# Class order of the pixels: from the ScalarE operands of a two-layer convolution kernel to its PSUM writes

## The chip, the cores and the metric

The kernel runs on one core of one Trainium2 chip. TensorE multiplies and writes PSUM, VectorE and ScalarE do elementwise work, GpSimd (POOL) and the SyncE queue (SP) move data. The metric is the device time of one execution in microseconds (us); lower is better.

## The reference

The input `x` is 16 images of 512 channels of 64 by 64 pixels, float32. Two layers follow each other, each `x = x + layer(groupnorm(x))`.

```python
# layer 0, on g = groupnorm(x)
corrs = [jnp.sum(g * shifted(g, di, dj), axis=1) for di in range(5) for dj in range(5)]
gs = jnp.stack(corrs, axis=1)                       # 25 products of a pixel with its 5x5 neighbours
gs = gs / jnp.sqrt(jnp.sum(gs * gs, axis=1, keepdims=True) + 1e-6)
feat = jnp.concatenate([g, gs], axis=1)             # 512 + 25 channels
x = x + relu(jnp.einsum('bchw,oc->bohw', feat, W) + bias)
# layer 1: each channel plane is max-pooled with one of the windows 1, 3, ... 13 that a small
# network on the plane means selects, two neighbouring windows are mixed, and x is added
```

## The kernel before

**Tiling.** An image lies in SBUF as 4 channel tiles (`CT`) of 128 partitions by 4096 pixels. Layer 0 goes through it in 8 chunks (`CH`) of 8 rows, 512 pixels each. Layer 1 starts when all images are through (about 2630 us) and is not touched by the change.

**One chunk of layer 0.** ScalarE normalises the chunk twice for each channel tile (`normalise`, L506 into the float32 `g32`, L508 into the float16 `gh`), and VectorE makes the low part `gl` = `g32` - `gh` (`low_parts`, L713). TensorE multiplies in three float16 products (high by high, high by low, low by high):

- `gram` (L1056): for each pair of image rows, 128 pixels as the weights and 256 pixels (4 rows) as the moving operand, 12 products that accumulate in a PSUM bank. Four such blocks belong to a chunk. VectorE masks the result to the band of neighbours (`mask`, L726, L731, L732) into `bq`.
- `turn_blocks` (L1114): transposes of four masked blocks, which ScalarE copies out (`after`, L528).
- `picks` (L1101): 48 small products that collect the 25 correlations from `bq`. `norm` (L1123) sums their squares, ScalarE takes the root (L537), VectorE divides (`descriptor`, L745, L749), POOL splits in high and low, and SP regroups the result with small DMAs into `tpair`.
- `conv` (L1079 to L1081): 48 products of 512 columns, 12 for each of the four output tiles. `tail` (L1134): 8 products of 256 columns that add the 25 descriptor channels of the chunk before to the same PSUM banks.
- ScalarE adds the bias and clips (`conv_out`, L520), VectorE adds the result to `x` and takes its statistics (`residual`, L738, L740).

**Order of the pixels.** A pair of rows has 128 pixels. In natural order their index is `(r, j, k)`: row, eight groups, pixel in the group. In class order it is `(k, r, j)`. Before, ScalarE makes the class order: both of its normalising instructions read `x` through `turned`, so that neighbouring elements lie 8 float32 apart, and write without a gap; L520 reads PSUM without a gap and writes `relu` with neighbouring elements 8 float32 apart. All of `gh`, `gl`, `g32` and the convolution's PSUM banks are in class order, and so are the rows and the columns of a Gram block. L1134 reads and writes in runs of 16 elements, L1101 in runs of 8.

**What sets the order.** Each engine has its program written out by hand; semaphores connect them. In iteration c TensorE issues: `picks`, a wait until the low parts of chunk c+2 are done (`s_gl`), Gram block 0 of chunk c+1, `norm`, Gram block 1, `tail` of chunk c-1, Gram blocks 2 and 3, convolution tile 0, the transposes, and convolution tiles 1 to 3. ScalarE issues: L535, L537, four L520, then `normalise` of chunk c+3 for the four channel tiles, with L528 between the second and the third. VectorE issues: mask 0, the descriptor, masks 1 to 3 with four `residual`s among them, and the low parts of chunk c+3. In iterations 0 to 3 it puts two statistics of the next image (L663) behind each low part, in iteration 0 also the aggregation of the last image's statistics (L793) ahead of them. In iteration 4 TensorE issues `group_average` (L1142) after convolution tile 1, and it waits there for L528.

Of the kernel before, what the change touches and what calls it, by code (L numbers as in the profile page):

```python
# [15 lines left out]
P = 128  # L16
C, H, W = 512, 64, 64
# [4 lines left out]
CW = ROWS * W  # L22
NB = H // 2
PAIRS = ROWS // 2
PRING = 2 * PAIRS
AFTER, SAME, BEFORE = range(3)
KS = 5
# [7 lines left out]
RING = 4  # L35
# [5 lines left out]
REP = 3 * 32  # L41
QUADS = 4
# [3 lines left out]
def const_arrays():  # L46


    p = np.arange(P)
    k, r, j = p // 16, p // 8 % 2, p % 8  # L50
    w = 8 * j + k
    band = (np.abs(w[:, None] - w[None, :]) <= KS // 2).astype(np.float32)


    pick = np.zeros((P, 3, 2, QUADS, 32), np.float32)
    for role in range(3):
        for e in range(2):
            for t in range(QUADS):
                di = r + 2 * (1 - role) - e
                rho = (k - 2 * t + 2) % 8  # L60
                ok = (np.abs(di) <= KS // 2) & (rho < 6)
                pick[p[ok], role, e, t, (rho * KS + di + 2)[ok]] = 1.0
    ssum = (p[:, None] // 32 == p[None, :] // 32).astype(np.float32) * 2.0 ** -12
    gavg = (p[:, None] // CG == p[None, :] // CG).astype(np.float32) / CG
    ident = np.eye(P, dtype=np.float32)
    before = (p[:, None] < p[None, :]).astype(np.float32)
    ones = np.ones((P, P), np.float32)
    return np.concatenate([band, pick.reshape(P, -1), ssum, gavg, ident, before, ones], axis=1)
# [18 lines left out]
def build(nc, x, wt, wturn, bias, w1t, b1, w2t, b2, consts, out):  # L87
    fp32, fp16, i32 = mybir.dt.float32, mybir.dt.float16, mybir.dt.int32
    ALU, ACT, AX = mybir.AluOpType, mybir.ActivationFunctionType, mybir.AxisListType
# [17 lines left out]
    with ctx:  # L107
# [3 lines left out]
        def sb(name, shape, dt):  # L111
            return ctx.enter_context(nc.sbuf_tensor(name, shape, dt))
# [3 lines left out]
        o = 0  # L116
        band = cst[:, o:o + P]; o += P
# [7 lines left out]
        bias_sb = sb("bias_sb", [P, CT], fp32)  # L125
# [10 lines left out]
        gbias = sb("gbias", [P, CT], fp32)  # L136
# [7 lines left out]
        def take(n):  # L144
            pos[0] += n
            assert pos[0] <= ARENA
            return arena[:, pos[0] - n:pos[0]]

        take(2 * CT * PIX)
        gh = take(CT * RING * CW // 2).bitcast(fp16).rearrange("p (t n) -> p t n", t=CT)  # L150
        gl = take(CT * RING * CW // 2).bitcast(fp16).rearrange("p (t n) -> p t n", t=CT)
        g32 = take(2 * CW).rearrange("p (s n) -> p s n", s=2)
# [7 lines left out]
        tpair = take(CW).bitcast(fp16).rearrange("p (s n) -> p s n", s=2)  # L160
        relu = take(2 * CW).rearrange("p (s n) -> p s n", s=2)
# [64 lines left out]
        psum = ctx.enter_context(nc.psum_tensor("psum", [P, 8, 512], fp32))  # L226
        GRAM0, BANK_A, BANK_N = 4, 6, 7
# [69 lines left out]
        def xs(ct, lo, n, par):  # L297

            return arena[:, bass.ds(par * (CT * PIX) + (ct * PIX + lo), n)]

        def turned(a):

            return a.rearrange("p (u r j k) -> p u k r j", r=2, j=8, k=8)

        def classed(a):

            return a.rearrange("p (u k r j) -> p u k r j", k=8, r=2, j=8)

        def gram_parts(t):


            parts, row = [], 2 * t
            while row < min(2 * t + 4, H):
                end = min(2 * t + 4, H, (row // (RING * ROWS) + 1) * RING * ROWS)
                parts.append(((row - 2 * t) * W, (row % (RING * ROWS)) * W, (end - row) * W))
                row = end
            return parts
# [170 lines left out]
        def _(act):  # L488
# [5 lines left out]
            def normalise(i, c, first=False, between=None):  # L494

                n0 = (i * CH + c) * CT
                act.wait_ge(s_newton, 3 * i + 3)
                if not first:

                    act.wait_ge(s_chunk_used, i * CH + c - RING + 1)  # L500
                for ct in range(CT):
                    if not (isinstance(n0, int) and n0 + ct < 2):
                        act.wait_ge(s_gl, n0 + ct - 1)
                    act.sem_inc(s_carry_a, 1)
                    piece = turned(xs(ct, c * CW, CW, i % 2))
                    act.activation(classed(g32[:, ct % 2, :]), piece, ACT.Identity, bias=gbias[:, ct:ct + 1],  # L506
                                   scale=grstd[:, ct:ct + 1])
                    act.activation(classed(gh[:, ct, (c % RING) * CW:(c % RING + 1) * CW]), piece, ACT.Identity,  # L508
                                   bias=gbias[:, ct:ct + 1], scale=grstd[:, ct:ct + 1]).then_inc(s_gh, 1)
                    if between and ct == 1:  # L510
                        between()

            def conv_out(chunk, o):
                n = chunk * CT + o
                act.wait_ge(s_conv, n + 1)
                if isinstance(n, int) and n < 2:
                    pass
                else:
                    act.wait_ge(s_added, n - 1)
                act.activation(turned(relu[:, o % 2, :]), classed(psum[:, o, :]), ACT.Relu, bias=bias_sb[:, o:o + 1],  # L520
                               scale=1.0 / (SC * SC)).then_inc(s_relu, 1)

            def after(i, c):
# [34 lines left out]
            for c in range(3):  # L558
                normalise(0, c, first=True)
# [6 lines left out]
            for o in range(CT):  # L566
                conv_out(B * CH - 1, o)
# [486 lines left out]
        def _(pe):  # L1054
            def product(dst, w, m, k, nk):
                return pe.matmul(dst, w, m, start=(k == 0), stop=(k == nk - 1))  # L1056

            def gram(i, t):
                if not (isinstance(i, int) and i == 0 and t < 2):
                    pe.wait_ge(s_masked, i * NB + t - 1)  # L1060
                own = ((2 * t) % (RING * ROWS)) * W
                for col, ring, n in gram_parts(t):
                    for ct in range(CT):
                        sh, sl = gh[:, ct, own:own + 2 * W], gl[:, ct, own:own + 2 * W]
                        mh, ml = gh[:, ct, ring:ring + n], gl[:, ct, ring:ring + n]
                        dst = psum[:, GRAM0 + t % 2, col:col + n]
                        product(dst, sh, mh, 3 * ct, 3 * CT)
                        product(dst, sh, ml, 3 * ct + 1, 3 * CT)
                        last = product(dst, sl, mh, 3 * ct + 2, 3 * CT)
                last.then_inc(s_gram, 1)  # L1070
# [34 lines left out]
            def turn_blocks(i, c):  # L1105

                pe.wait_ge(s_masked, i * NB + PAIRS * (c + 1))

                if isinstance(i, int) and i == 0 and c == 0:
                    pe.wait_ge(s_vchain, STATS_CHAIN)  # L1110
                else:
                    pe.wait_ge(s_root, i * CH + c)
                for t in range(PAIRS * c, min(PAIRS * (c + 1), NB - 1)):
                    last = pe.transpose(psum[:, BANK_N, (t % PAIRS) * P:(t % PAIRS + 1) * P],  # L1114
                                        bq[:, BEFORE, ((t + 1) % PRING) * P:((t + 1) % PRING + 1) * P], ident)
                last.then_inc(s_turned, 1)

# [7 lines left out]
            def tail(i, c):  # L1125


                half = c % 2
                pe.wait_ge(grouped[half], (i * (CH // 2) + c // 2 + 1) * GROUPED)
                src = tpair[0:REP, half, :].rearrange("p (t q u s) -> p q u t s", t=QUADS, q=2, u=PAIRS)  # L1130
                for o in range(CT):
                    dst = psum[:, o, :].rearrange("p (u t q s) -> p q u t s", u=PAIRS, t=QUADS, q=2)
                    for par in range(2):
                        last = pe.matmul(dst[:, par], wd[0:REP, par * C + o * P:par * C + (o + 1) * P],  # L1134
                                         src[:, par], start=False, stop=True, skip_group_check=True)
                    last.then_inc(s_conv, 1)
# [43 lines left out]
            for t in range(PAIRS):  # L1180

                pe.wait_ge(s_gl, (2 if t == PAIRS - 1 else 1) * CT)
                gram(0, t)
            turn_blocks(0, 0)
            image(0, False)
            if B > 2:
                with pe.Fori(1, B - 1) as i:
                    image(i, False)
            image(B - 1, True)
            tail(B - 1, CH - 1)  # L1190


# [9 lines left out]
            for ct in range(CT):  # L1202
                last = product(psum[0:HID, 2, 0:B], w1_sb[:, ct, :], gap[:, :, ct], ct, CT)
            last.then_inc(s_smm, 1)
            pe.wait_ge(s_sstat, 4)
            for ct in range(CT):
                last = pe.matmul(psum[:, 3, ct * B:(ct + 1) * B], w2_sb[0:HID, ct * P:(ct + 1) * P], hid[0:HID, :],
                                 start=True, stop=True)
# [76 lines left out]
```

## Time and profile before

| | us |
|---|---|
| median of 3 runs | 4609.29 |
| lowest and highest | 4605.99 and 4613.17 |
| the profiled execution's own time | 4614.89 |
| its span, first to last instruction | 4613.1 |

The time outside the span is 1.8 us. In a row, "PE" is TensorE, "PEld" its weight load, "DVE" VectorE, "ACT" ScalarE; L12 is line 12 of the kernel. A duration of a matmul includes the time in which it overlaps the next one, so the distance from start to start tells the rate. "[1.4 <-DVE L713]" behind a row is idle time of its engine ahead of it, and what ended that.

### The profile page before, as it was taken

What the parts mean: (1) busy time and instruction counts of PE and PEld (TensorE: products, weight loads), DVE (VectorE), ACT (ScalarE), POOL (GpSimd) and SP (SyncE); (2) the same over time, 40 slices, a digit from 0 to 9 for tenths busy, and PEclk for the clock granted to TensorE, in tenths of its full rate; (3) what the DMA queues carried; (4) which work ended last, traced back from release to release, by engine and by line L of the source; (5) the groups of instructions that cost most, each with busy time, mean ns of one, the idle gap of its engine ahead of it and who ended that gap; (6) DMA issues with size and microseconds to landing.
All of it is one profiled execution on the core that took longest, in us unless ns stands there. A gap on an engine that the chain in (4) does not pass through costs nothing. (4 is left out here: it accounts for less than half of the span.)

```text
span 4613.1 us, 73329 instructions
## 1 busy us (share of the span) xinstructions
PE 3847.0 (83%) x23656; PEld 2135.8 (46%) x23657; DVE 3520.3 (76%) x4010; ACT 2589.7 (56%) x2830; POOL 637.1 (14%) x624
## 2 busy tenths in 40 slices
PE   3999999999999999999989767898888777777665
PEld 2655555555555555555556443343333333323222
DVE  5676667667666765766665576899999999999994
ACT  4777777777777777777777434443333233232322
POOL 0000000000000000000000012333232322222221
PEclk9999999999999999999999878898899888888887
DMA  4233322323333232333321246553333333323221
GB/s 167 97 116 116 109 103 100 134 98 116 116 116 111 99 120 97 116 116 116 115 98 61 61 129 217 180 182 154 146 147 134 132 143 125 134 107 123 111 119 48
DMA packets 174313, 556.98 MB, mean 121 GB/s; under 512 B 91248, under 2 KB 91248, under 8 KB 157552
## 3 DMA queue, kind: packets, MB, share of 16 engines
q1 hardware_dynamic: 152016, 283.62, 17.7%
q0 software_dynamic: 21920, 268.59, 15.1%
q8 instruction: 206, 3.38, 0.3%
q14 instruction: 171, 1.40, 0.1%
HBM read 277.23 MB, written 274.86 MB: 120 GB/s over the span
## 5 line engine op out<-in xcount | busy, mean ns | idle before, releaser
L931 DVE TENSOR_TENSOR arena<-arena 128x2048 f32<-128x2048 f32 (+4 forms) x730 | 1759.1, 2430 | 107.7 <-ACT arena L579 66.3
L1250 PE MATMUL psum<-arena 128*128 128x512 f32 x1072 | 615.0, 658 | 442.0 <-issue 399.0
L1056 PE MATMUL psum<-arena 128*128 128x256 f16 (+1 forms) x6344 | 744.2, 272 | 152.7 <-DVE arena L713 134.8
L579 ACT ACTIVATE arena<-arena 128x4096 f32<-128x4096 f32 x67 | 244.2, 3645 | 972.3 <-DVE arena L931 706.6
L1079 PE MATMUL psum<-arena 128*128 128x512 f16 x2048 | 782.3, 382 | 0.7 <-ACT arena L520 0.7
L1080 PE MATMUL psum<-arena 128*128 128x512 f16 x2048 | 782.3, 382 | 0.0
L1081 PE MATMUL psum<-arena 128*128 128x512 f16 x2048 | 782.1, 382 | 0.0
L520 ACT ACTIVATE arena<-psum,bias_sb 128x512 f32<-128x512 f32 x512 | 577.5, 1184 | 270.6 <-PE psum L1134 171.3
L1056 PEld LDWEIGHTS psum<-arena 128*128 128x128 f16 x6344 | 597.4, 99 | 241.5 <-issue 124.1
L713 DVE TENSOR_TENSOR arena<-arena 128x512 f16<-128x512 f32 x512 | 351.7, 687 | 432.0 <-ACT arena L508 431.9
L506 ACT ACTIVATE arena<-arena,gbias,grstd 128x512 f32 (+1 forms) x512 | 669.3, 1307 | 6.0 <-DVE arena L713 4.7
L508 ACT ACTIVATE arena<-arena,gbias,grstd 128x512 f16 (+1 forms) x512 | 668.6, 1306 | 0.0
L1254 PE MATMUL psum<-arena 128*128 128x512 f32 x1072 | 579.9, 624 | 0.0
L1250 PEld LDWEIGHTS psum<-arena 128*128 128x128 f32 x1072 | 217.7, 210 | 738.3 <-issue 674.3
L599 ACT ACTIVATE arena<-psum,arena 128x512 f32<-128x512 f32 x536 | 336.0, 689 | 321.8 <-PE psum L1254 321.4
L1252 PE MATMUL psum<-arena 128*128 128x512 f32 x896 | 500.7, 642 | 0.0
L738 DVE TENSOR_TENSOR arena<-arena 128x512 f32 (+1 forms) x512 | 349.4, 682 | 141.8 <-ACT arena L520 141.8
L740 DVE BATCH_NORM_STATS2 bny<-arena 128x6 f32 (+1 forms) x512 | 355.4, 694 | 98.2 <-DVE arena L738 96.0
L409 POOL CAST arena<-arena 128x128 f16<-128x128 f32 x128 | 37.4, 292 | 2510.4 <-DVE arena L749 2510.4
L1254 PEld LDWEIGHTS psum<-arena 128*128 128x128 f32 x1072 | 219.2, 204 | 290.1 <-issue 290.1
L663 DVE BATCH_NORM_STATS2 bnx<-arena 128x6 f32 (+1 forms) x512 | 326.2, 681 | 11.3 <-DMA arena<-in_x 11.2
L1081 PEld LDWEIGHTS psum<-arena 128*128 128x128 f16 x2048 | 201.6, 98 | 245.5 <-issue 7.0
(138 smaller groups left out, 2672.0 us busy)
## 6 DMA issues: line engine op xcount, KB each, us to landing
arena<-in_x SPq DMA_DIRECT2D x64, 2048.0 KB, 12.6
y_planes<-arena SPq DMA_DIRECT2D x64, 2048.0 KB, 7.9
arena<-arena SPq DMA_DIRECT2D x1536, 8.0 KB, 1.7
arena<-plane_records,arena POOLq DMA_INDIRECT x67, 3.0
arena<-y_planes,arena POOLq DMA_INDIRECT x67, 9.4
out<-arena POOLq DMA_INDIRECT x67, 8.7
arena<-in_wt SPq DMA_DIRECT2D x1, 1024.0 KB, 12.6
cst<-in_consts SPq DMA_DIRECT2D x1, 768.0 KB, 4.3
```

Of the source, the lines that this page charges most:

```text
L506: act.activation(classed(g32[:, ct % 2, :]), piece, ACT.Identity, bias=gbias[:, ct:ct + 1], scale=grstd[:, ct:ct + 1])
L508: act.activation(classed(gh[:, ct, (c % RING) * CW:(c % RING + 1) * CW]), piece, ACT.Identity, bias=gbias[:, ct:ct + 1], scale=grstd[:, ct ...
L520: act.activation(turned(relu[:, o % 2, :]), classed(psum[:, o, :]), ACT.Relu, bias=bias_sb[:, o:o + 1], scale=1.0 / (SC * SC)).then_inc(s_ ...
L740: dve.bn_stats(bny[:, o, c, :], y).then_inc(s_y, 1)
L931: ins = dve.tensor_tensor(dst, a, b, ALU.max)
L1056: return pe.matmul(dst, w, m, start=(k == 0), stop=(k == nk - 1))
L1079: pe.matmul(dst, h, gh[:, ct, slot], start=(ct == 0), stop=False)
L1080: pe.matmul(dst, h, gl[:, ct, slot], start=False, stop=False)
L1081: last = pe.matmul(dst, l, gh[:, ct, slot], start=False, stop=(ct == CT - 1))
L1250: pe.matmul(dst, diag[:, s, 0, :], bufs[:, u, b * CW:(b + 1) * CW], start=True, stop=False)
L1252: pe.matmul(dst, diag[:, s, 1, :], small[:, s, b * ROWS:(b + 1) * ROWS, 1:W + 1], start=False, stop=False)
L1254: pe.matmul(dst, diag[:, s, 2, :], big[:, s, b * CW:(b + 1) * CW], start=False, stop=True)\
```

## The change

The number and the order of the instructions stay the same on every engine, and so do the bytes that are read and written. What changes is where operands are read and written:

- ScalarE, L506 and L508: they read `x` and write `g32` and `gh` in natural order, without a gap.
- ScalarE, L520: it reads PSUM and writes `relu` without a gap.
- TensorE, Gram (L1056): the 128 or 256 moving columns are natural pixels, read without a gap. The PSUM destination goes through the new `classed`, so that each next column is written 16 float32 (64 bytes) from the last, and after 8 columns the pattern moves on. The rows of a Gram block (its PSUM partitions) are in natural order, its columns in class order as before.
- TensorE, the transposes (L1114): the 128 columns are written through the same pattern.
- TensorE, `tail` (L1134): it reads runs of 64 elements instead of 16, and writes PSUM with each next column 8 float32 (32 bytes) from the last instead of in runs of 16.
- `conv` reads and writes as before, without a gap, now in natural order.
- `picks` (L1101) has the same access patterns; only the constants `pick` and `band` change, since the Gram rows are natural and the transposed blocks are not.

```diff
-    k, r, j = p // 16, p // 8 % 2, p % 8
-    w = 8 * j + k
-    band = (np.abs(w[:, None] - w[None, :]) <= KS // 2).astype(np.float32)
+    w_col = 8 * (p % 8) + p // 16
+    band = (np.abs(p[:, None] % W - w_col[None, :]) <= KS // 2).astype(np.float32)
...
+        r, k = (p // 8 % 2, p // 16) if role == AFTER else (p // W, p % 8)
...
-        def turned(a):
-
-            return a.rearrange("p (u r j k) -> p u k r j", r=2, j=8, k=8)
-
         def classed(a):
 
-            return a.rearrange("p (u k r j) -> p u k r j", k=8, r=2, j=8)
+            return a.rearrange("p (u k r j) -> p u r j k", k=8, r=2, j=8)
...
-                    piece = turned(xs(ct, c * CW, CW, i % 2))
-                    act.activation(classed(g32[:, ct % 2, :]), piece, ACT.Identity, bias=gbias[:, ct:ct + 1],
+                    piece = xs(ct, c * CW, CW, i % 2)
+                    act.activation(g32[:, ct % 2, :], piece, ACT.Identity, bias=gbias[:, ct:ct + 1],
                                    scale=grstd[:, ct:ct + 1])
-                    act.activation(classed(gh[:, ct, (c % RING) * CW:(c % RING + 1) * CW]), piece, ACT.Identity,
+                    act.activation(gh[:, ct, (c % RING) * CW:(c % RING + 1) * CW], piece, ACT.Identity,
...
-                act.activation(turned(relu[:, o % 2, :]), classed(psum[:, o, :]), ACT.Relu, bias=bias_sb[:, o:o + 1],
+                act.activation(relu[:, o % 2, :], psum[:, o, :], ACT.Relu, bias=bias_sb[:, o:o + 1],
...
-                        dst = psum[:, GRAM0 + t % 2, col:col + n]
+                        dst = classed(psum[:, GRAM0 + t % 2, col:col + n])
...
-                    last = pe.transpose(psum[:, BANK_N, (t % PAIRS) * P:(t % PAIRS + 1) * P],
+                    last = pe.transpose(classed(psum[:, BANK_N, (t % PAIRS) * P:(t % PAIRS + 1) * P]),
...
-                src = tpair[0:REP, half, :].rearrange("p (t q u s) -> p q u t s", t=QUADS, q=2, u=PAIRS)
+                src = tpair[0:REP, half, :].rearrange("p (t q s) -> p q t s", t=QUADS, q=2)
...
-                    dst = psum[:, o, :].rearrange("p (u t q s) -> p q u t s", u=PAIRS, t=QUADS, q=2)
+                    dst = psum[:, o, :].rearrange("p (s t q) -> p q t s", t=QUADS, q=2)
```

## Rows read from the trace of the kernel before

**Rows 1.** the page: busy time, and the span in 40 slices
```profile
PE 3847.0 (83%) x23656; PEld 2135.8 (46%) x23657; DVE 3520.3 (76%) x4010; ACT 2589.7 (56%) x2830; POOL 637.1 (14%) x624
...
PE   3999999999999999999989767898888777777665
...
ACT  4777777777777777777777434443333233232322
...
PEclk9999999999999999999999878898899888888887
```

**Rows 2.** all lines of the program: line, engine, operation, count, busy us, mean ns, idle
```profile
L1056 PE MATMUL psum<-arena 128*128 128x256 f16 (+1 forms) x6344 | 744.2, 272 | 152.7 <-DVE arena L713 134.8 <-DVE arena L726 15.4 <-DVE arena L825 2.5
L506 ACT ACTIVATE arena<-arena,gbias,grstd 128x512 f32 (+1 forms) x512 | 669.3, 1307 | 6.0 <-DVE arena L713 4.7 <-DVE gbias L703 1.3
L508 ACT ACTIVATE arena<-arena,gbias,grstd 128x512 f16 (+1 forms) x512 | 668.6, 1306 | 0.0
...
L520 ACT ACTIVATE arena<-psum,bias_sb 128x512 f32<-128x512 f32 x512 | 577.5, 1184 | 270.6 <-PE psum L1134 171.3 <-DVE arena L738 87.9 <-issue 0.2
...
L599 ACT ACTIVATE arena<-psum,arena 128x512 f32<-128x512 f32 x536 | 336.0, 689 | 321.8 <-PE psum L1254 321.4
...
L579 ACT ACTIVATE arena<-arena 128x4096 f32<-128x4096 f32 x67 | 244.2, 3645 | 972.3 <-DVE arena L931 706.6 <-issue 183.3 <-DMA arena<-y_planes,arena 82.4
...
L1134 PE MATMUL psum<-arena 96*128 96x256 f16 x1024 | 133.0, 272 | 0.0
```

**Rows 3.** whom TensorE waited for, 100 to 2630 us: total, times, longest
```profile
PE psum L1056 <- DVE arena L713: 121.4, 81, 1.9
PE psum L1101 <- issue: 33.4, 15, 3.0
PE psum L1142 <- ACT arena L528: 26.4, 15, 1.8
```

**Rows 4.** stretches (us, us): busy of PE, PEld, DVE, ACT, POOL, clock, DMA share, GB/s
```profile
1538.27:1557.81 19.54, 18.12 (x159) 11.51 (x159) 15.32 (x27) 15.07 (x15) 0.72 (x2) 1.00 0.56 209
1596.98:1619.39 22.41, 20.46 (x162) 12.33 (x162) 13.41 (x31) 15.15 (x15) 0.72 (x2) 0.92 0.43 153
1619.39:1637.45 18.06, 18.06 (x166) 11.47 (x159) 10.53 (x21) 14.52 (x15) 0.72 (x2) 1.00 0.16 56
1637.45:1656.95 19.50, 17.53 (x163) 10.75 (x158) 11.15 (x19) 15.78 (x17) 0.72 (x2) 1.00 0.37 121
1678.32:1698.38 20.06, 18.13 (x165) 11.43 (x159) 15.45 (x31) 15.49 (x16) 0.72 (x2) 1.00 0.34 114
```

**Rows 5.** TensorE in order of time, chunks 1 and 2 of an image
```profile
1538.27 1.48 PE L1056 MATMUL psum<-arena 128*128 128x256 f16 x12 [1.92 <-DVE arena L713]
...
1539.81 1.47 PE L1056 MATMUL psum<-arena 128*128 128x256 f16 x12
1541.12 1.04 PE L1134 MATMUL psum<-arena 96*128 96x256 f16 x8
...
1547.21 0.60 PE L1114 MATMUL psum<-cst,arena 128*128 128x128 f32 x4
...
1557.81 1.48 PE L1056 MATMUL psum<-arena 128*128 128x256 f16 x12 [1.42 <-DVE arena L713]
```

**Rows 6.** VectorE in order of time, chunk 2 of that image
```profile
1569.51 0.68 DVE L713 TENSOR_TENSOR arena<-arena 128x512 f16<-128x512 f32 x1
...
1571.30 0.68 DVE L713 TENSOR_TENSOR arena<-arena 128x512 f16<-128x512 f32 x1
```

**Rows 7.** VectorE in order of time, chunk 0 of the next image
```profile
1691.61 0.69 DVE L713 TENSOR_TENSOR arena<-arena 128x512 f16<-128x512 f32 x1
...
1697.56 0.69 DVE L713 TENSOR_TENSOR arena<-arena 128x512 f16<-128x512 f32 x1 [0.48 <-ACT arena L508]
```

**Rows 8.** TensorE in order of time, in chunk 4
```profile
1611.27 0.39 PE L1142 MATMUL psum<-aggx,cst 128*128 128x4 f32 x2 [1.79 <-ACT arena L528]
...
1612.33 0.63 PE L1081 MATMUL psum<-arena 128*128 128x512 f16 x1
```

## The prediction

> **What bounds the kernel now.** I read the page first [rows 1]. In the 40 slices TensorE shows 9 tenths from slice 2 to slice 23 with ScalarE at 7: this is layer 0, up to about 2630 us. Behind it the change touches nothing, so those 1985 us stay. Within layer 0 the digit 9 hides what matters: does TensorE wait at all, and for whom? The table of waits answers [rows 3]: from 100 to 2630 us the Gram products (L1056) wait 121.4 us in 81 places for the low parts (L713), `group_average` (L1142) waits 26.4 us for ScalarE's copy L528, and 33.4 us are waits for nothing that the trace shows, once per image. The low parts themselves come late because of ScalarE: its two normalising instructions take 1307 and 1306 ns for 512 elements and L520 takes 1184, where L599, a contiguous instruction of the same size in layer 1, takes 689 [rows 2].
>
> Then the periods. From a Gram start to the next, TensorE is busy 18.12 of 19.54 us in chunk 1, all 18.06 of 18.06 in chunk 5, 17.53 of 19.50 in chunk 6 and 18.13 of 20.06 in chunk 0 [rows 4]. So the kernel is TensorE's stream of 18.1 us a chunk, plus 1.4 to 1.9 us of waiting for ScalarE in about five chunks of eight. Two prices hang on that: what ScalarE gets faster can bring back the waits and no more, and what TensorE gets slower counts in full.
>
> **The change, part 1: ScalarE reads and writes without gaps.** In each chunk 12 instructions (four each of L506, L508, L520) go from about 1.31 and 1.18 us to about 0.69 (L599; its operands are PSUM to SBUF, the sort of L520, and I take it for L506 and L508 too) [rows 2]. That is 8 x 0.62 + 4 x 0.50 = 7.0 us of ScalarE's 15.1 us in a chunk of 19.5 [rows 4]. What is late next? VectorE. In chunk 2 its first low part starts at 1569.51, 11.70 us behind the Gram start of 1557.81 [rows 5, 6]; the first L520 ahead of that chain ends 0.5 us sooner, which makes 11.2. From one low part to the next is 1.79 us where nothing is waited for (1569.51 to 1571.30) [rows 6]. The last of four then ends at 11.2 + 3 x 1.79 + 0.69 = 17.3 us, and 0.13 later the next Gram can start (as from 1697.56 + 0.69 to 1698.38) [rows 4, 7]. That is 17.4, below TensorE's 18.1, so in chunks 1 to 3 the wait of 1.42 us [rows 5] or a little more goes entirely: 4.3 us. In chunk 0 VectorE has the aggregation ahead: 1691.61 - 1678.32 - 0.5 + 6.2 = 19.0 us [rows 4, 7], so of the wait of 1.93 us only 1.06 go. In chunks 5 to 7 VectorE has no statistics to do, and one wait goes, that of chunk 6: 19.50 - 18.1 = 1.4. In chunk 4 the wait for L528 (1.79) goes, and with it what it brings: right behind it the matmuls take 0.63 instead of 0.38 us, the distance of starts is 425 instead of 215 ns for eight of them, that is TensorE at 1.2 instead of 2.4 GHz, and the stretch has a mean granted clock of 0.92 [rows 4, 8]; that costs 8 x 0.21 = 1.7. In all 1.06 + 4.3 + 1.4 + 3.5 = 10.3 us of an image. From the table of waits instead: 121.4 + 26.4 + 15 x 1.7 - 15 x 0.87 = 160 us, and the 10.3 over 15.5 images give the same. I take **160**. Ahead of the loop three chunks are normalised, 12 pairs of L506 and L508; each pair gets 1.2 us shorter, VectorE's 0.69 stays hidden, and some of TensorE's Gram work comes behind: **10** of the 15 us. Sum of this part: -170 us. Only if TensorE's own stream stays as it is.
>
> **Part 2: TensorE writes PSUM with gaps.** Now a Gram matmul of 256 columns starts 0.109 us behind the last: (1.47 - 0.27) / 11 [rows 2, 5], one column per cycle of 2.4 GHz. `tail` is at (1.04 - 0.27) / 7 = 0.110, though it writes in runs of 16. No row has neighbouring columns apart. How many are to be written so: Gram 31 blocks of 256 and one of 128 columns, 12 products, 16 images, makes 1.548 million columns; `tail` 1024 x 256 = 0.262 million. Together 1.81 million columns, 754 us at one cycle each. The price in extra cycles per column is what decides.
> Lower bound: zero. It can't be below, since the contiguous stream already moves a column in every cycle. Upper bound: what gaps cost ScalarE. Its contiguous rate is (3645 - 689) / (4096 - 512) = 0.825 ns per element with 266 ns fixed; with gaps in what it writes, (1184 - 266) / 512 = 1.79 ns, 2.2 times as much; with gaps in what it reads, (1307 - 266) / 512 = 2.03 ns, 2.5 times [rows 2]. Had TensorE the same factor, that would be 1.2 to 1.5 extra cycles, 900 to 1130 us. If it were the same nanoseconds instead (1.2 extra on 1.81 million columns), 2200 us; I leave that out of the range as the far end. I take one extra cycle, a factor of 2: the row nearest to it is the one where an engine writes 4-byte elements 32 bytes apart, as `tail` will, and that is the 2.2; a stream of one column per cycle loses whole cycles. This is **+754 us**. The transposes (496 of 128 columns) I cost at nothing: four of them take 0.60 us in all [rows 5], 0.11 each behind the first, that is two cycles per column, so a write slot is spare; if not, +53.
> The Trainium skill, "PSUM — Partial Sum Buffer", Specifications, says that PSUM lines are 8 bytes and that any access pattern with gaps slows matmuls significantly. Literally taken the trace contradicts it: `tail` writes with gaps between its runs of 16 at 0.110 us, no slower than Gram [rows 5]. "Advanced Engine Details and Errata", Memory Cachelines, is closer: every two consecutive elements should be adjacent. Runs of 16 and of 8 obey that, and the new patterns do not. By that rule one column would take the place of two, which I estimate at the same 754 us; without the rule the rows leave zero to 1130 open.
> The reads: contiguous before and after for Gram and `conv`, longer runs for `tail`; nothing. L713, the masks, L738 read contiguous operands before and after; nothing. No DMA, no wait and no semaphore changes.
>
> **The sum for the forecast.** With 18.1 + 48 x 0.107 + 8 x 0.107 = 24.1 us per chunk TensorE is far behind ScalarE (8 us) and VectorE (19.0 at most), so all waits and the clock dip in chunk 4 go too, the 0.87 us in chunk 0 included: -173 and -10. 4614.9 + 754 - 183 = 5186 us against the profiled execution. The median lies 5.6 us under that execution: **5180 us**, 12% slower.
>
> **Rivals.** (a) Gaps in PSUM writes are free for TensorE. Then part 1 stands alone: 4614.9 - 170 - 5.6 = 4439 us. For it: `tail` shows that jumps between runs cost nothing, and no row shows a matmul held up by its write. Against it: this chip's memory does charge ScalarE for gaps, both reading and writing. This one is nearly as likely as the forecast. It is 3.7% faster and turns round at 170 / 754 = 0.23 extra cycles per column; above that the kernel is slower. (b) The write costs a part of a cycle, 0.25 to 0.85: 4620 to 5070 us. Against it: nothing in the rows shows a half price. (c) The write costs ScalarE's factor or more: 1.2 extra cycles give 5330, 1.5 give 5560. (d) ScalarE's gain isn't what L599 says, since L506 and L508 read SBUF with two per-partition operands. At 0.9 us each ScalarE has 10.5 us a chunk, still less than VectorE, so (a) moves by under 20 us. (e) The gain and the price cancel: needs 0.2 to 0.26 extra cycles, a narrow strip.
>
> **How the numbers follow.** Forecast (0.85 to 1.15 extra cycles, transposes with or without a price: 5070 to 5320) 0.42; (a) 0.40, with 4435 to 4500 for most of it; (b) 0.07; (c) 0.08; (e) 0.03. The forecast's own range is 5070 to 5320. For 8 in 10 the range has to take in (a), so it is 4430 to 5320 with 0.11 left out. Faster by over 0.2% is 0.41, within 0.2% (about what a measurement of this kernel can tell from no change) 0.03, slower 0.56.
>
> **What would show it.** In the profile after, L506, L508 and L520 at about 690 ns say that part 1 holds (in either case). Twelve Gram matmuls as one row of 2.6 instead of 1.47 us, and `tail`'s eight of 1.8 instead of 1.04, say that the forecast is right; 1.47 and 1.04 say (a). TensorE's waits for L713 should be near 0, or 13 us in (a), all in chunk 0. The period of chunk 5, now 18.06 without a wait, is the cleanest single number: 24.1 in the forecast, 18.1 in (a). Wrong would be both if `conv` (0.38 us, untouched) changed its rate, or if the masks of VectorE, which wait for Gram, became the new wait.

## The result

The changed kernel takes 5156.42 us (median of 4 runs, 5146.46 to 5166.05), the kernel before 4611.23 us (4 runs). The ratio is 1.118, with a 95% interval of 1.115 to 1.121: 12% slower. The profiled execution took 5166.05 us, its span is 5164.3 us.

The page of the changed kernel, the lines that answer to [rows 1] (its own lines are numbered 3 less from L503 on: L503, L505, L517 are L506, L508, L520 of before, L1053 the Gram products, L1131 the tail, L710 the low parts):

```profile
PE 4568.3 (88%) x23656; PEld 2456.0 (48%) x23657; DVE 3560.3 (69%) x4010; ACT 1891.1 (37%) x2830; POOL 638.4 (12%) x624
...
PE   5999999999999999999999998679988877767675
...
ACT  2433433433433334334334341444333333222221
...
PEclk9999999999999999999999997789989988888887
```

ScalarE fell from 7 tenths to between 3 and 4 in layer 0, and by 699 us in all. TensorE's 9 tenths, which ended at slice 20 with an 8 and a last 9 behind (the prediction read them up to slice 23), now last without a break to slice 24, and each slice is 129 us instead of 115. The groups of lines show both halves of the change, as in [rows 2] (mean ns behind the busy time):

```profile
L1053 PE MATMUL psum<-arena 128*128 128x256 f16 (+1 forms) x6344 | 1394.7, 414 | 16.0 <-DVE arena L710 9.5 <-DVE arena L723 4.0 <-DVE arena L822 2.5
...
L503 ACT ACTIVATE arena<-arena,gbias,grstd 128x512 f32 (+1 forms) x512 | 412.4, 806 | 134.4 <-DVE arena L710 133.1 <-DVE gbias L700 1.3
L505 ACT ACTIVATE arena<-arena,gbias,grstd 128x512 f16 (+1 forms) x512 | 409.6, 800 | 0.0
...
L517 ACT ACTIVATE arena<-psum,bias_sb 128x512 f32<-128x512 f32 x512 | 337.8, 685 | 737.3 <-DVE arena L735 382.5 <-PE psum L1131 354.8
...
L1131 PE MATMUL psum<-arena 96*128 96x256 f16 x1024 | 247.2, 421 | 0.0
```

ScalarE's instructions went from 1307, 1306 and 1184 ns to 806, 800 and 685. A Gram product went from 272 to 414 ns and a tail product from 272 to 421. In the table of waits from 100 to 3150 us, where [rows 3] had 121.4 us for the low parts and 26.4 for L528, one line is left:

```profile
PE psum L1098 <- issue: 34.3, 18, 2.9
```

So TensorE waits for no other engine any more (these 34.3 us without a visible cause were 33.4 before), and the kernel got slower by 545 us. The rows in order of time say how ([rows 5]):

```profile
1556.54 2.77 PE L1053 MATMUL psum<-arena 128*128 128x256 f16 x12
...
1561.91 1.93 PE L1131 MATMUL psum<-arena 96*128 96x256 f16 x8
...
1571.45 0.60 PE L1111 MATMUL psum<-cst,arena 128*128 128x128 f32 x4
```

Twelve Gram products take 2.77 instead of 1.48 us, the tail 1.93 instead of 1.04. The stretches from one Gram start to the next, as in [rows 4], for chunk 4 and chunk 5 (stretch, busy time of PE, PEld, DVE, ACT, POOL, then the granted clock):

```profile
1532.27:1556.54 24.27, 24.27 (x169) 14.47 (x163) 12.29 (x27) 9.89 (x16) 0.72 (x2) 1.00 0.32 107
1556.54:1580.56 24.02, 24.02 (x165) 13.88 (x159) 11.62 (x22) 9.62 (x15) 0.72 (x2) 1.00 0.20 77
```

Chunk 5, which waited for nothing before, went from 18.06 to 24.02 us with TensorE busy all the time.

The granted clock is 1.00 in both stretches, but it still falls elsewhere. Where the images change, behind the wait without a visible cause, stands this:

```profile
1629.65 0.43 PE L1098 MATMUL psum<-arena,cst 128*32 128x64 f32 x16 [2.41 <-issue]
1630.01 4.45 PE L1053 MATMUL psum<-arena 128*128 128x256 f16 x12
```

```profile
1630.01:1634.52 4.51, 4.51 (x21) 2.70 (x15) 0.02 (x1) 0.28 (x1) 0.00 (x0) 0.62 0.01 4
```

From 1630.01 to 1634.52 the mean granted clock is 0.62, and the twelve products take 4.45 instead of 2.77 us. In layer 0 the trace has nine such places in the changed kernel, with 37.5 us at half the clock in all.

### The profile page after: what moved, and what is told of

Read it like the earlier page. It is cut to its first block and busy times, and to the rows that moved or that the text cites. A ratio compares the mean times of both kernels' runs of the same rounds, so it can differ in the third digit from the quotient of the medians.

```text
span 5164.3 us, 73329 instructions
## 1 busy us (share of the span) xinstructions
PE 4568.3 (88%) x23656; PEld 2456.0 (48%) x23657; DVE 3560.3 (69%) x4010; ACT 1891.1 (37%) x2830; POOL 638.4 (12%) x624
## 5 line engine op out<-in xcount | busy, mean ns | idle before, releaser
L928 DVE TENSOR_TENSOR arena<-arena 128x2048 f32<-128x2048 f32 (+4 forms) x730 | 1759.4, 2430 | 112.1 <-ACT arena L576 70.0
L1053 PE MATMUL psum<-arena 128*128 128x256 f16 (+1 forms) x6344 | 1394.7, 414 | 16.0 <-DVE arena L710 9.5
L1053 PEld LDWEIGHTS psum<-arena 128*128 128x128 f16 x6344 | 842.5, 137 | 448.9 <-issue 18.0
L723 DVE TENSOR_TENSOR arena<-psum,cst 128x256 f32<-128x256 f32 x448 | 190.1, 425 | 880.1 <-PE psum L1053 880.1
L517 ACT ACTIVATE arena<-psum,bias_sb 128x512 f32<-128x512 f32 x512 | 337.8, 685 | 737.3 <-DVE arena L735 382.5
L503 ACT ACTIVATE arena<-arena,gbias,grstd 128x512 f32 (+1 forms) x512 | 412.4, 806 | 134.4 <-DVE arena L710 133.1
L710 DVE TENSOR_TENSOR arena<-arena 128x512 f16<-128x512 f32 x512 | 344.0, 682 | 134.4 <-ACT arena L505 134.4
L505 ACT ACTIVATE arena<-arena,gbias,grstd 128x512 f16 (+1 forms) x512 | 409.6, 800 | 0.0
```

The costliest lines, as they stand in the source:

```text
L503: act.activation(g32[:, ct % 2, :], piece, ACT.Identity, bias=gbias[:, ct:ct + 1], scale=grstd[:, ct:ct + 1])
L505: act.activation(gh[:, ct, (c % RING) * CW:(c % RING + 1) * CW], piece, ACT.Identity, bias=gbias[:, ct:ct + 1], scale=grstd[:, ct:ct + 1]) ...
L928: ins = dve.tensor_tensor(dst, a, b, ALU.max)
```

## Experiment 1: each part alone

The theory is that of the prediction: gaps in a float16 product's PSUM writes cost one extra cycle per column, and ScalarE's part alone is a gain. The rivals are that something else in the change slows TensorE, that the price depends on the distance, and that the float32 transposes pay too. The three strided destinations of the changed kernel were made contiguous, all or all but one:

```diff
-                        dst = classed(psum[:, GRAM0 + t % 2, col:col + n])
+                        dst = psum[:, GRAM0 + t % 2, col:col + n]
...
-                    last = pe.transpose(classed(psum[:, BANK_N, (t % PAIRS) * P:(t % PAIRS + 1) * P]),
+                    last = pe.transpose(psum[:, BANK_N, (t % PAIRS) * P:(t % PAIRS + 1) * P],
...
-                    dst = psum[:, o, :].rearrange("p (s t q) -> p q t s", t=QUADS, q=2)
+                    dst = psum[:, o, :].rearrange("p (t q s) -> p q t s", t=QUADS, q=2)
```

No gaps at all:

> The changed kernel with the PSUM destinations of the Gram products, the transposes and the tail without gaps. The pixels of the Gram blocks and of the descriptor end up in the wrong order, so this part of the result is another; the number of instructions and of columns is the same. ScalarE's part of the change alone is left. Theory (gaps in PSUM writes cost TensorE one extra cycle per column and nothing else got slower): 4440 us, Gram at 0.109 us per product, period of chunk 5 18.1 us, L503 to L517 as in the changed kernel (0.81, 0.80, 0.69 us). Rival (something else of the change slows TensorE, such as the natural order or ScalarE's faster accesses to SBUF): over 4620 us, and Gram products stay above 0.15 us.

Gaps only in the Gram products:

> The changed kernel with gaps only in the Gram products; transposes and tail write without gaps (their part of the result is in another order). Theory of one extra cycle per column: 48 x 0.103 us more per chunk than without gaps, 645 us for 1.548 million columns, less what still hides behind the last 13 us of waits: 5040 us. Tail 0.110 us, Gram 0.212 us per product. Rival (the price belongs to the tail or to the transposes more than to the column count): under 4900 us.

Gaps only in the tail:

> The changed kernel with gaps only in the tail (8 float32 apart); Gram products and transposes write without gaps (their part of the result is in another order). Theory: 0.262 million columns at one extra cycle are 109 us more than without gaps at all: 4550 us, tail at 0.215 us per product, Gram at 0.109. Rival (the cost grows with the distance, 32 bytes being cheaper than 64): under 4520 us and tail under 0.18 us per product.

Gaps only in the transposes:

> The changed kernel with gaps only in the transposes; Gram and tail write without gaps (their part of the result is in another order). Theory (a float32 transpose takes two cycles per column anyway, and a gap costs up to two cycles per column in all): no difference to the kernel without any gaps, 4440 us, four transposes as one row of 0.60 us. Rival (a gap adds a cycle to whatever a column takes): 496 x 0.053 = 26 us more, 4466 us, and a row of 0.76 us.

| kernel | median, us | ratio to before, 95% interval | last tail product starts at, us |
|---|---|---|---|
| before | 4608.54 | | 2623.2 |
| no gaps | 4401.12 | 0.956 (0.955 to 0.958) | 2421.1 |
| Gram alone | 5042.06 | 1.095 (1.093 to 1.097) | 3054.5 |
| tail alone | 4501.41 | 0.977 (0.975 to 0.978) | 2525.3 |
| transposes alone | 4402.30 | 0.956 (0.954 to 0.957) | 2422.8 |
| the change (against 4611.23) | 5156.42 | 1.118 (1.115 to 1.121) | 3170.7 |

The last column is the end of layer 0 in the profile. It is the cleaner one, because layer 1 is not the same in all of these kernels. Where the Gram blocks are in a wrong order, layer 1 runs 880 instead of 896 of the products that were L1252 before, and from the last tail product to the end it takes 4397.6 - 2421.1 = 1976.5 us with no gaps and 1982.5 with gaps in the tail alone. Where they are right it takes 4613.1 - 2623.2 = 1989.9 us before, 1993.6 with the change and 1982.5 with gaps in the Gram products alone. So it differs by up to 17 us, and not by the order alone. In layer 0 the Gram products' gaps cost 633.4 us, the tail's 104.2, the transposes' 1.7; together 739, and with all three 749.6. ScalarE's part alone gains 202.1 us.

Of the 10 us by which the whole is dearer than its parts, some 7.5 are waits counted twice. Without gaps the Gram products still wait 11.8 us for L710 (100 to 2430 us); gaps in the Gram products hide all of it, gaps in the tail all but 4.3, and both together can't hide it twice. So the three destinations are the whole price; the last 3 us aren't traced.

Three of the four totals were forecast too high, because the kernel without gaps was put at 4440 us and took 4401. By its total of 4501 us the tail alone would even fall to its rival (under 4520 us); what decides is the distance from the kernel without gaps, 100 us where 109 were forecast, and the tail's own rate.

The two forms side by side. With no gaps, in order of time:

```profile
1507.46 1.48 PE L1053 MATMUL psum<-arena 128*128 128x256 f16 x12
...
1510.31 1.04 PE L1131 MATMUL psum<-arena 96*128 96x256 f16 x8
```

With gaps only in the tail, 32 bytes between columns:

```profile
1516.72 1.47 PE L1053 MATMUL psum<-arena 128*128 128x256 f16 x12
1518.03 1.89 PE L1131 MATMUL psum<-arena 96*128 96x256 f16 x8
```

From start to start that is (1.89 - 0.42) / 7 = 0.210 us for 256 columns at 32 bytes. For the Gram products at 64 bytes, the block behind the row of 2.77 us above takes 2.75:

```profile
1559.36 2.75 PE L1053 MATMUL psum<-arena 128*128 128x256 f16 x12
```

That is (2.75 - 0.42) / 11 = 0.212. Between 32 and 64 bytes the distance doesn't matter. Four transposes stay at one row of 0.60 us, with gaps or without. The rival of one more cycle for any column falls; that the gap fits in the second of a float32 column's two cycles agrees with this, but isn't shown by itself.

## Experiment 2: what counts as a gap

The tail of the kernel before wrote in runs of 16 at full rate, so a jump by itself is not the cost. Is it the missing neighbour? Three kernels write the Gram columns in other patterns, with transposes and tail contiguous as above:

```diff
-                        dst = classed(psum[:, GRAM0 + t % 2, col:col + n])
+                        dst = psum[:, GRAM0 + t % 2, col:col + n].rearrange("p (k m e) -> p m k e", k=8, e=2)       # pairs
...
+                        dst = psum[:, GRAM0 + t % 2, 1 + col:1 + col + n].rearrange("p (k m e) -> p m k e", k=8, e=2)  # one element on
...
+                        dst = psum[:, GRAM0 + t % 2, col:col + n].rearrange("p (m e) -> p e m", e=2)                # 8 bytes apart
```

> The changed kernel without gaps in transposes and tail, and with the Gram columns written as pairs: two neighbouring columns 4 bytes apart on an 8-byte boundary, the next pair 128 bytes further (64 for the blocks of 128). The order of the pixels in the Gram blocks is another. Theory A (TensorE writes two neighbouring float32 at a time, and a lone one costs as much as two): Gram 0.109 us per product, as without gaps, 4440 us in all. Theory B (any step back or forth costs a cycle, once per run): 0.109 + 128 x 0.00042 = 0.163 us per product and 4700 us. Theory C (only runs of a full 8 or 16 elements are free): 0.21 us and 5040 us.

> As the kernel with pairs, with every pair starting one element later, so that its two elements lie in two different aligned 8-byte words; the masks read one element later too. Theory A (aligned words of 8 bytes): 0.212 us per Gram product, as in the changed kernel, 5040 us. Rival (any two adjacent elements go together, aligned or not): 0.109 us, 4440 us.

> As the kernel with pairs, with neighbouring columns 8 bytes apart: first all even elements, then all odd ones. Theory A (aligned words of 8 bytes): 0.212 us per Gram product, 5040 us, the same as with 64 bytes. Rival (lines of 16 bytes or more, or a price that grows with the distance): between 0.109 and 0.19 us.

They took 4400.99, 5043.18 and 5046.40 us (one run each). The same twelve products in order of time, pairs on 8-byte boundaries:

```profile
1507.92 1.47 PE L1053 MATMUL psum<-arena 128*128 128x256 f16 x12
```

Pairs one element further on:

```profile
1503.30 2.75 PE L1053 MATMUL psum<-arena 128*128 128x256 f16 x12
```

Single columns 8 bytes apart:

```profile
1501.44 2.75 PE L1053 MATMUL psum<-arena 128*128 128x256 f16 x12
```

This settles the rule as far as times can. An aligned pair goes out at 0.109 us per 256 columns with a jump of 64 or 128 bytes behind every pair; the same pair shifted by 4 bytes, or single columns only 8 bytes apart, cost the full 0.212. The times of all these patterns are those of one aligned 8-byte word every 0.83 ns (0.212 us / 256): two columns in one word are free, one column in a word costs as much as two. The page "Advanced Engine Details and Errata" of the Trainium skill, section Memory Cachelines, gives PSUM lines of 8 bytes and says that every two consecutive elements should be contiguous; the trace agrees, and the shifted pairs (0.212 instead of 0.109 us) show that the pair has to lie in one line. The page "PSUM — Partial Sum Buffer" of the Trainium skill, section Specifications, says that any access pattern with gaps slows matmuls significantly; the run with pairs (1.47 us, nothing lost) contradicts "any".

## Experiment 3: could the reads make the order instead?

If TensorE read its moving operand with gaps for nothing, the class order could come from there. And would ScalarE be content with pairs?

```diff
-                        mh, ml = gh[:, ct, ring:ring + n], gl[:, ct, ring:ring + n]
+                        mh, ml = (a[:, ct, ring:ring + n].rearrange("p (u r j k) -> p u k r j", r=2, j=8, k=8) for a in (gh, gl))  # 16 bytes apart
...
+                        mh, ml = (a[:, ct, ring:ring + n].rearrange("p (m e) -> p e m", e=2) for a in (gh, gl))    # 4 bytes apart
...
-                    piece = xs(ct, c * CW, CW, i % 2)
+                    piece = xs(ct, c * CW, CW, i % 2).rearrange("p (s t q) -> p t s q", t=4, q=2)      # ScalarE reads pairs
```

> The changed kernel without gaps in any PSUM write; the moving operand of the Gram products is read from SBUF with gaps instead (float16 elements 16 bytes apart, in the order of the kernel before). Theory (SBUF charges TensorE for gaps too, as it does ScalarE): 0.2 us or more per Gram product, about 5040 us or more. Rival (TensorE's reads are wide enough that gaps are free): 0.109 us, 4440 us; then the class order could be had from the reads.

> The changed kernel without gaps in PSUM writes, with the moving operand of the Gram products read from SBUF 4 bytes apart (every second float16; first all even, then all odd pixels); the order of the pixels in the Gram blocks is another. With 16 bytes between elements a Gram product took about 0.34 us at 2.4 GHz and 0.455 at 1.2. Theory (SBUF serves lines of 16 bytes, so four elements of a line still come together): 0.109 us per product and 4400 us. Rival (any gap in a read costs): 0.2 us or more per product, over 5000 us.

> The changed kernel without gaps in PSUM writes, with ScalarE's two normalising instructions reading x in pairs: two neighbouring float32, then a jump of 32 bytes to the next pair. They write without a gap; the order of the pixels is another. Contiguous they take 0.81 and 0.80 us, with single elements 32 bytes apart 1.31. Theory (SBUF charges by the line as PSUM does, and a pair is enough): 0.81 us and 4400 us. Rival (a jump costs by itself): 1.05 us, and 4400 to 4450 us, since ScalarE has slack.

The first took 6835.98 us. Two rows of twelve products, and then three stretches: around either row, and from 1500 to 4800 us:

```profile
1531.55 5.58 PE L1053 MATMUL psum<-arena 128*128 128x256 f16 x12
1537.35 5.61 PE L1053 MATMUL psum<-arena 128*128 128x256 f16 x12
```

```profile
1531.60:1537.00 5.40, 5.40 (x16) 1.60 (x14) 0.00 (x0) 0.28 (x1) 0.00 (x0) 0.85 0.54 218
1537.40:1542.80 5.40, 5.40 (x14) 1.52 (x13) 1.43 (x3) 0.37 (x1) 0.72 (x2) 0.50 0.03 5
...
1500.00:4800.00 3300.00, 3276.51 (x14073) 1258.76 (x14072) 1186.99 (x2128) 834.79 (x1322) 63.26 (x176) 0.68 0.16 56
```

A product takes about (5.6 - 0.6) / 11 = 0.455 us instead of 0.109, four times as much, and the same at a granted clock of 0.85 and of 0.50. On top of that the granted clock falls to a mean of 0.68, though TensorE is busy 3276.5 of 3300 us. It falls within the row that starts at 1531.55, while TensorE is busy, and it stays at half behind the Gram products: the contiguous `conv` products behind them take 0.63 instead of 0.38 us, as they do behind this row of the same kernel.

```profile
1510.18 8.33 PE L1053 MATMUL psum<-arena 128*128 128x256 f16 x24
...
1518.73 0.63 PE L1077 MATMUL psum<-arena 128*128 128x512 f16 x1
```

So a product whose reads are 16 bytes apart takes twice as long as one whose writes have gaps (0.212 us). The 0.34 us "at 2.4 GHz" in the text for the second run were wrong: they are this row of 24 divided by 24, but twelve of its products have only 128 columns, and its granted clock is 0.50.

With 4 bytes between the elements the kernel took 4443.31 us and twelve products 1.53 us:

```profile
1510.98 1.53 PE L1053 MATMUL psum<-arena 128*128 128x256 f16 x12
```

That is (1.53 - 0.27) / 11 = 0.115 us per product, 5% over contiguous. The rival of 0.2 us falls, but the reads aren't quite free either: layer 0 is 35 us longer than without gaps. With ScalarE reading pairs, 4397.93 us:

```profile
L503 ACT ACTIVATE arena<-arena,gbias,grstd 128x512 f32 (+1 forms) x512 | 434.3, 848 | 141.4 <-DVE arena L710 139.3 <-DVE gbias L700 1.3 <-issue 0.3
```

848 ns with pairs, 806 contiguous, 1307 with single elements in the kernel before. So ScalarE's reads of SBUF, too, take aligned pairs nearly as fast as a contiguous row; pairs off the 8-byte boundary were not tried there.

## Experiment 4: a kernel that beats both

Natural pixels `(r, j, k)` with k = 2t + q have neighbours that differ in q only. A class order `(t, r, j, q)` keeps those pairs together, so the Gram products can go from one order to the other in aligned pairs. The masks, the picks and the constants follow; ScalarE stays as in the changed kernel, and the tail keeps its gaps, since it writes the pixels of one q alone.

```diff
-    w_col = 8 * (p % 8) + p // 16
+    w_col = 8 * (p // 2 % 8) + 2 * (p // 32) + p % 2
...
-        r, k = (p // 8 % 2, p // 16) if role == AFTER else (p // W, p % 8)
+        r, k = (p // 16 % 2, 2 * (p // 32) + p % 2) if role == AFTER else (p // W, p % 8)
...
-                        dst = classed(psum[:, GRAM0 + t % 2, col:col + n])
+                        dst = psum[:, GRAM0 + t % 2, 0:2 * P].rearrange("p (t n) -> p t n", t=4)[:, :, col // 4:(col + n) // 4]\
+                            .rearrange("p t (s q) -> p s t q", q=2)
...
-                            .rearrange("p (u t q r j) -> p t r q u j", t=QUADS, q=2, r=2, j=8)
+                            .rearrange("p (u t r j q) -> p t r u j q", t=QUADS, q=2, r=2, j=8)
...
-                                .rearrange("p (q u r j) -> p r q u j", q=2, r=2, j=8)
+                                .rearrange("p (q u r j) -> p r u j q", q=2, r=2, j=8)
```

> A kernel made from what the runs so far show. ScalarE stays in natural order. A new class order keeps pairs of neighbouring pixels together, so that the Gram products are written as aligned pairs; the masks, the picks and the constants follow it. The tail keeps its gaps of 32 bytes. The picks now read runs of 16 elements and write PSUM with gaps (float32, two cycles per column). Theory: Gram 0.109 us per product, tail 0.211, picks as one row of 0.88 us as before; the kernel with gaps only in the tail took 4501 us, and layer 1 takes 13 us more with the right classes: 4510 to 4520 us, 2% faster than the kernel before. Rival (float32 products into 32 partitions also pay for gaps): picks over 1.2 us, 4560 us or more.

It took 4509.15 us (4 runs, 4498.64 to 4515.67), ratio 0.979 (0.976 to 0.981): 2.1% faster than the kernel before (surely faster; whether by 2% the interval leaves open) and 12.6% faster than the change. In order of time:

```profile
1511.94 0.88 PE L1104 MATMUL psum<-arena,cst 128*32 128x64 f32 x48
1512.75 1.48 PE L1058 MATMUL psum<-arena 128*128 128x256 f16 x12
...
1515.61 1.89 PE L1137 MATMUL psum<-arena 96*128 96x256 f16 x8
```

The Gram row is back at 1.48 us. The 48 picks now write PSUM with gaps and still take 0.88 us: float32 again. What is left is the tail's 0.85 us per chunk, the 104 us of experiment 1. In this kernel layer 1 takes 1981.3 us, so the 13 us that its forecast added for layer 1 were not there to see; layer 0 ends at 2520.4 us.

## Why the prediction was right

**The bound.** "TensorE's stream of 18.1 us a chunk, plus waiting" held on both sides: without gaps chunk 5 takes 18.05 us (in the stretches below), with all gaps 24.02, where the forecast said 18.1 and 24.1.

**The price of a gap.** The forecast of one extra cycle came to 754 us for 1.81 million columns; layer 0 shows 749.6. The bounds left this open between 0 and 1130 us, and what chose the value was ScalarE's row with gaps in its writes, a factor of 2.2, rounded to whole cycles. The number was right; as an argument the likeness was weaker than the number. Experiment 2 shows a rule of aligned pairs, and ScalarE's own cost of a gap in the same terms is (1184 - 685) / 512 = 0.97 ns per element, more than the 0.40 ns that TensorE pays. Rival (a) had 0.40 and wasn't refuted by any row of the kernel before. That the price was a whole cycle and not nothing was a nearly even bet, and that it came out was in part luck. The 749.6 us also hold two things that the product of columns and cycles doesn't: the clock is at half for 37.5 us in layer 0 instead of 17.1 without gaps, which I estimate at 10 us (six times the 1.7 us of the row at 1630.01), and the 11.8 us of waits that the gaps hide work the other way.

**The transposes.** Costed at nothing because of their two cycles per column: 1.7 us measured. Right, and the float32 picks of experiment 4 agree with the reason given.

**ScalarE's part.** Forecast -170 us, and 4439 us for rival (a), which is what the kernel without gaps is. Measured -202.1 us in layer 0 and 4401 us. The direction and the place were right; terms of the sum were too small. Five stretches of that kernel (from Gram start to Gram start, chunks 0, 4, 5, 6 and 7):

```profile
1397.96:1416.92 18.96, 18.11 (x164) 11.46 (x159) 15.36 (x31) 9.90 (x16) 0.72 (x2) 1.00 0.31 108
1471.11:1489.41 18.30, 18.30 (x167) 12.10 (x163) 12.81 (x30) 9.78 (x16) 0.72 (x2) 1.00 0.32 111
1489.41:1507.46 18.05, 18.05 (x164) 11.50 (x159) 11.13 (x22) 9.51 (x15) 0.72 (x2) 1.00 0.37 133
1507.46:1524.71 17.25, 17.25 (x163) 10.78 (x158) 10.37 (x18) 9.40 (x15) 0.72 (x2) 1.00 0.29 104
1524.71:1545.08 20.37, 18.20 (x164) 11.52 (x158) 10.48 (x18) 9.51 (x15) 0.72 (x2) 1.00 0.38 134
```

Chunk 0 went from 20.06 to 18.96, a gain of 1.10 where 1.06 was forecast: VectorE is indeed what is late next, with 0.85 us of waiting left. In chunks 1 to 3 the wait went as said. Chunk 4 went from 22.41 to 18.30, 4.1 us instead of 3.5: the wait for L528 and the stretch at 1.2 GHz behind it are both gone (clock 1.00, before 0.92). The rest is a wait of 0.16 us for a mask (L732) ahead of the transposes and 2.16 us less busy time (20.46 to 18.30) where 1.7 was forecast. Chunk 6 went from 19.50 to 17.25, 2.25 instead of 1.4: I measured it against the 18.1 us of the other chunks, but its last Gram block is half as wide, and [rows 4] had shown 17.53 us of busy time. Chunk 7 gained 1.0 us in this image, where I gave it nothing; before it was

```profile
1656.95:1678.32 21.37, 18.27 (x158) 11.47 (x159) 10.56 (x18) 14.88 (x14) 0.72 (x2) 1.00 0.27 101
```

Its gap without a cause in the trace, 2.96 us, is 2.17 in the kernel without gaps; why, is not shown, and it isn't so in every image: the tables of waits have 33.4 us of these gaps before and 30.5 without gaps, 3 us in all.

Over the whole of layer 0 the tables of waits and the clock give this account of the 202.1 us. The waits for the low parts fell from 121.4 to 11.8 us and those for L528 from 26.4 to nothing, as forecast. Waits that the forecast left out (TensorE for the masks and for `group_spread`, 5.2 and 3.6 us, and two smaller ones) fell from 9.9 to 0.6, the gaps without a cause by 3. The time at half the clock fell from 71.7 to 17.1 us, worth 27 us where 15 x 1.7 was forecast, and the first tail product starts 11.5 us sooner (102.4 to 90.9), where 10 was. That makes 187 us. The last 15 stand in TensorE's busy time, mostly in chunk 4 (0.46 us beyond the clock) and chunk 6 (17.53 to 17.25); what they are is not shown.

**L506 and L508 at L599's time.** They take 806 and 800 ns, not 689. Rival (d) had allowed up to 0.9 us and said that it would not matter; it doesn't, because ScalarE is busy 9.5 of 18 us.

**The sum.** 5186 us were forecast for the profiled execution and 5166.05 measured. The forecast booked the last 13 us of waits to ScalarE's part, while the experiments count them against the price. Booked its way, with the 11.8 us measured, ScalarE's part is 214 us where 183 were forecast, and the price 761 us where 754 were. That is 24 us less in layer 0 than forecast; layer 1 took 4 us more than before. So the price was right to 1%, and the 20 us are ScalarE's part.

## What to carry over

An engine that waits 1.4 us of 19.5 for another can win back little more than that (the rest here was mainly clock: 27 us), and a cycle added to the engine that sets the pace counts in full: here 202 us of gain stood against 750 us of price, and the balance point was at 0.27 extra cycles per column. When a layout change moves a permutation to another engine, write down for each access what the innermost runs are, and aim for pairs of 4-byte elements on 8-byte boundaries; a permutation that keeps pairs together was free on TensorE's PSUM writes (1.47 us for twelve products) and nearly free on ScalarE's reads (848 instead of 806 ns). Price a pattern that the trace doesn't contain with a small run before rewriting constants around it.

## What was not expected of the hardware

- Aligned pairs with a jump behind every pair write PSUM at the full rate of float16 products (1.47 us for twelve), a shift of 4 bytes doubles the time (2.75 us). I had reckoned with a factor, not with such a sharp condition.
- Reading the moving operand with 16 bytes between float16 elements costs four times the contiguous time (0.455 against 0.109 us), and the granted clock falls to 0.68 on average over a stretch in which TensorE is busy 3276.5 of 3300 us. What makes the clock fall is not shown; TensorE was not idle ahead of it.
- The float32 products and transposes of this kernel write PSUM with gaps for nothing (0.60 us for four transposes, 0.88 us for 48 picks, in both forms).
- Not tried: a layout in which the tail also writes aligned pairs. It needs neighbours in PSUM of the same q; as `tpair` is laid out, these are pixels that ScalarE would have to fetch 32 bytes apart.
